# Shifted attention scores on masks preset by ScalarE and VectorE, in fixed pairs of PSUM banks

## The chip, the cores and the metric

The kernel runs on one core of a Trainium2 chip. The metric is the device time of one execution in microseconds. The median of three runs of the kernel before is 666.25 us (665.54 to 667.37).

## The reference

One block of a transformer with adaptive layer norms, on x of 4 batch rows x 512 tokens x 256 features, all in float32:

- `mod = silu(c) @ wmod` gives six vectors per batch row: two shifts, two scales, two gates.
- `h = layernorm(x) * (1 + ca) + sa`, then an attention block on h: rmsnorm, a projection to q, k and v with 32 heads of 8 features, rotary embedding of q and k, scores `q k^T / sqrt(8)`. A score is masked where the key is later than the query or lies in another of the four blocks of 128 tokens; then softmax, `@ v`, the output projection, and a gated MLP of width 512 with its own rmsnorm. `x += ga * result`.
- `h = layernorm(x) * (1 + cb) + sb`, then a gated feed-forward of width 704 with low-rank experts: a softmax router over 8 experts picks two of rank 16, and the result is `x += gb * (...)`.

For this change only the attention scores matter. Since the mask cuts the sequence into four blocks of 128 tokens, each of 32 heads in each of four blocks is a causal 128 x 128 softmax.

## The kernel before

A program written out engine by engine: each engine has its own instruction stream in source order, and semaphores (`Signal`) join them. The four batch rows are processed one after another, with the preparation of the next row woven into the current one.

**Attention units.** A row has `UNITS` = 8 units: two halves of the heads (16 heads) times four blocks of 128 tokens. A unit handles 16 heads as four groups of four heads, two groups at a time: `n = 2u + a` with a in 0, 1 counts the parts. For each part TensorE computes the scores twice.

- `scores_for_max` (L1546): two mask matmuls (`masked`, L1531: identity x mask in bf16, 512 columns, `start=True`) and two score matmuls of K = 32 in different row tiles, from rounded q and k, into one pair of PSUM banks. VectorE (`unit_max`, L1135) reduces 1024 columns to 8 negated maxima. When both parts are done, TensorE transposes the maxima (`max_transposed`, L1564, four 128-column transpositions) and ScalarE copies them as additional rows into the stacked queries (`max_to_rows`, L773). These scores run `AHEAD` = 2 units ahead.
- `shifted_scores` (L1579): with the maxima in the contraction (K = 100), again two mask matmuls and two score matmuls of 512 columns into a pair of banks. ScalarE takes the exponential of 1024 columns into `prob[a]` (L807; in units 6 and 7 the first part in two halves, L802 and L804).
- `contexts` (L1598): 16 matmuls of 128 columns in column tiles of width 32 per part (the trace counts 64 per unit and not 32, since each float32 matmul is issued twice) accumulate values and denominators in bank 6. VectorE's `normalise` (L1151) takes a reciprocal and a product.
- GpSimd spreads queries, keys and values for units to come (`spread_queries`, L570).

**Slots.** Three pairs of banks serve as slots (`slot`, L360): slot 0 is banks 2 and 3, slot 1 banks 4 and 5, slot 2 banks 0 and 1. The list `fills` (L349 to L357) has every use of a slot in TensorE's order: maximum scores `s1`, transposition `t`, shifted scores `s2`. Before, they rotate through the three slots. `fill` (L1522) makes TensorE wait until the earlier use of the same slot was read: `max_done` (VectorE) for s1, `max_rows` (ScalarE) for t, `exp_done` (ScalarE) for s2.

**TensorE's order in a unit.** Shifted scores of part 0, maximum scores (two units ahead) of part 0, the same two for part 1, contexts of part 0, contexts of part 1, transposition of the maxima. After that: in unit 2 the mean of the next row (L1437), in unit 4 its mean of squares, in unit 5 the spreading of its 1/std (not in the last row).

**The other queues in a unit.** ScalarE: two exponentials; in unit 0 a copy of h; `max_to_rows`; in row 0 further casts in units 0 and 1 (`high_parts`, `chunk_high`); in units 3 and 6 the squares of the next row (`front_squares`, L706), which wait for VectorE's centring. VectorE: two reductions; in row 0, unit 2, `chunk_low`; in unit 3 `centre` (L1042), in unit 6 `front_scale`; then `normalise`.

Of the kernel before, what the change touches and what calls it, by code (L numbers as in the profile page):

```python
# [32 lines left out]
P = 128  # L33
# [69 lines left out]
CHUNK_WIDTHS += [SPLIT_COLS - sum(CHUNK_WIDTHS) - 2 * S, 2 * S]  # L103
CHUNKS = [(sum(CHUNK_WIDTHS[:c]), width) for c, width in enumerate(CHUNK_WIDTHS)]
LATE_CHUNK = 4
FIRST_CONST = CONST["ident"][0]


# [53 lines left out]
def adaln_kernel(nc, x, smalls, wmod, wsplit, wplain, consts, masks, out):  # L162
    with ExitStack() as ctx:
# [167 lines left out]
        lora_hi = signal("lora_hi", 4)  # L331
        powers_set = signal("powers_set", 1)
        exp_half = signal("exp_half", 2)
        lora_lo = signal("lora_lo", 4)
        gu_ready = signal("gu_ready", FT * VARIANTS)
        ff_silu = signal("ff_silu", FT * VARIANTS)
# [14 lines left out]
        for u in range(UNITS):  # L351
            for a in range(2):
                fills += [("s2", 2 * u + a)] + ([("s1", 2 * (u + AHEAD) + a)] if u + AHEAD < UNITS else [])
            if u + AHEAD < UNITS:
                fills += [("t", u + AHEAD)]
        for n, what in enumerate(fills[6:]):
            slot_of[what] = (n + 2) % 3  # L357
        freed_by = {"s1": max_done, "t": max_rows, "s2": exp_done}

        def slot(fill):  # L360
# [307 lines left out]
        def _(act):  # L668
# [104 lines left out]
            def max_to_rows(row, u, ahead):  # L773
# [4 lines left out]
                nc.scalar.copy(q_st[MROW:KS, half * GQ:(half + 1) * GQ, blk * P:(blk + 1) * P], src)\  # L778
                    .then_inc(max_rows.sem, 1)

            def tails_stacked():

                act.wait_ge(chunk_hi[5].sem, 1)
                act.wait_ge(chunk_lo[5].sem, 1)
                for name, width in (("wd", D), ("ad", E * R)):
                    at = KEPT[name] + (FT - 1) * width
                    nc.scalar.copy(w_lo[TAIL:P, at:at + width], w_hi[0:TAIL, at:at + width].bitcast(F32))\
                        .then_inc(tail_stacked.sem, 1)

            def row_steps(row, last):  # L790

                for u in range(UNITS):
                    for a in range(2):
                        n = 2 * u + a
                        act.wait_ge(s2_ready.sem, s2_ready.count(row, n + 1))
                        if n >= 2:

                            act.wait_ge(pv_done.sem, pv_done.count(row, n - 1))
                        scores = slot(("s2", n)).rearrange("p a s -> p (a s)")
                        if u + AHEAD >= UNITS and a == 0:  # L800

                            nc.scalar.activation(prob[a][:, 0:S], scores[:, 0:S], ACT.Exp, scale=SCALE)\  # L802
                                .then_inc(exp_half.sem, 1)
                            nc.scalar.activation(prob[a][:, S:2 * S], scores[:, S:2 * S], ACT.Exp, scale=SCALE)\  # L804
                                .then_inc(exp_done.sem, 1)
                        else:
                            nc.scalar.activation(prob[a], scores, ACT.Exp, scale=SCALE).then_inc(exp_done.sem, 1)  # L807
                        if row == n == 0:
                            max_to_rows(0, 1, 0)
                    if u == 0:  # L810

                        act.wait_ge(out_ready.sem, out_ready.count(row, 0))
                        act.wait_ge(front.shifted.sem, front.shifted.count(row, 1))
                        nc.scalar.copy(h[:], h_next[:]).then_inc(h_moved.sem, 1)
                    if u + AHEAD < UNITS:
                        max_to_rows(row, u + AHEAD, 0)
                    if row == 0:

                        if u == 0:
                            act.wait_ge(rope_hi.sem, 4)  # L820
                            high_parts(3)
                            high_parts(2)
                        elif u == 1:
                            chunk_high(LATE_CHUNK)
                        elif u == 4:
                            tails_stacked()
                    if not last and u in (3, 6):
                        front_squares(row, 0 if u == 3 else 1, 1)
# [145 lines left out]
        def _(dve):  # L974
# [172 lines left out]
            def row_steps(row, is_last):  # L1147
# [19 lines left out]
                for u in range(UNITS):  # L1167
                    if not is_last and u == 5:
                        variance(0, row)
                    if u + AHEAD < UNITS:  # L1170
                        unit_max(row, u + AHEAD, 0)
                    if row == 0 and u == 2:
                        chunk_low(LATE_CHUNK)
                    if not is_last:
# [241 lines left out]
        def _(pe):  # L1416
# [160 lines left out]
            def row_steps(row, is_last):  # L1577

                def shifted_scores(n):  # L1579
                    u, a = n // 2, n % 2  # L1580
                    blk, half = u % BLOCKS, u // BLOCKS
                    if a == 0:
# [3 lines left out]
                            half_stacked(pe, row, half, 0)  # L1586
                        if u == BLOCKS:
                            pe.wait_ge(ones_back.sem, 16)
                    to = fill(row, "s2", n, 0)
                    for g in range(2):  # L1590
                        masked(to[:, g, :], 2)
                    for g in range(2):
                        gq = 2 * a + g
                        last = nc.tensor.matmul(to[:, g, :], k_st[0:KS, half * GQ + gq, blk * P:(blk + 1) * P],  # L1594
                                                q_ex[u % 2][0:KS, gq], start=False, stop=True)
                    last.then_inc(s2_ready.sem, 1)

                def contexts(n):  # L1598
# [29 lines left out]
                    shifted_scores(0)  # L1628
                max_transposed(row, 1, 0)
                for u in range(UNITS):  # L1630
                    for a in range(2):
                        if row or u or a:
                            shifted_scores(2 * u + a)
                        if u + AHEAD < UNITS:
                            scores_for_max(row, 2 * (u + AHEAD) + a, 0)
                    for a in range(2):
                        contexts(2 * u + a)
                    if u + AHEAD < UNITS:
                        max_transposed(row, u + AHEAD, 0)
                    if not is_last:  # L1640

# [384 lines left out]
```

## Time and profile before

| | |
|---|---|
| median of 3 runs | 666.25 us (665.54 to 667.37) |
| the profiled execution | 665.03 us, of which the span is 663.2 us |
| TensorE's mean granted clock | 0.978 of full speed |
| TensorE | 619.9 us busy, 93% of the span, 5816 matmuls |
| TensorE's weight loads | 424.9 us, beside its matmuls |
| VectorE | 404.6 us, 61%, 623 instructions |
| ScalarE | 315.7 us, 48%, 478 instructions |
| GpSimd | 185.2 us, 28%, 264 instructions |
| mask matmuls (L1532) | 256, 77.9 us busy |

Times are microseconds unless marked ns. A matmul's duration in the trace holds the latency of the array, and matmuls overlap: what one costs is the distance from its start to the next one's start. In the view in order of time, a row gives the start, the time until the group's end, the engine and the line; in brackets is the idle time of the engine before it and what ended it. "PE" is the matmul and "PEld" the load of its weights.

### The profile page before, as it was taken

Reading aid. Unit: us, or ns where it says so; the run is one execution under the profiler, and the core shown is the slowest. Engines: PE = TensorE matmul, PEld = TensorE weight load, DVE = VectorE, ACT = ScalarE, POOL = GpSimd, SP = SyncE. Lnnn points to the kernel's source line nnn. Section 1 sums busy time; section 2 is a strip of 40 time slices with the busy share of each in tenths; the row PEclk is TensorE's granted clock in tenths of the full one; section 3 lists DMA queues with packets and bytes.
Section 4 is the critical chain, followed back from the end, with each engine's and each line's share of the span. In section 5 each row is a group of like instructions: output and inputs, shape, how many; then the busy total and the mean of one; then the engine's idle time right before and its main releaser. Section 6 shows DMA issues by size and latency. Waiting matters only on the chain.

```text
span 663.2 us, 13983 instructions
## 1 busy us (share of the span) xinstructions
PE 619.9 (93%) x5816; PEld 424.9 (64%) x5816; DVE 404.6 (61%) x623; ACT 315.7 (48%) x478; POOL 185.2 (28%) x264
## 2 busy tenths in 40 slices
PE   5689999999999999999999999999999999869996
PEld 3545667567864667667884657766785566637783
DVE  2786744687467563668557555468647664447554
ACT  3736464356444356257443445437534444417442
POOL 1156640024016561034005662023102763000000
PEclk8599999999999999999999999999999999989999
DMA  8744000034022000025012100004202100000000
GB/s 327 239 111 119 30 3 1 1 83 109 1 60 99 2 2 3 0 48 144 1 27 70 64 3 2 1 14 123 57 0 64 65 2 3 1 1 0 1 1 32
DMA packets 16456, 31.77 MB, mean 48 GB/s; under 512 B 5060, under 2 KB 5828, under 8 KB 16260
## 3 DMA queue, kind: packets, MB, share of 16 engines
q1 hardware_dynamic: 14856, 27.98, 14.5%
q0 software_dynamic: 1152, 2.36, 1.4%
q8 instruction: 46, 0.75, 0.5%
q10 hardware_dynamic: 384, 0.52, 0.3%
q14 instruction: 18, 0.15, 0.1%
HBM read 12.99 MB, written 2.10 MB: 23 GB/s over the span
## 4 chain that ended last, share of the span: by engine, by line
PE 72%; DVE 14%; ACT 9%; issue 4%; DMA 1%; DVEq 0%; SPq 0%; ACTq 0%
PE bank L1622 8%; PE bank L1532 7%; PE bank L1424 5%; PE bank L1428 5%; PE bank L1425 5%; PE bank L1710 4%; PE bank L1560 3%; PE bank L1594 3%; PE bank L1805 3%; PE bank L1807 3%; PE bank L1568 3%; PE bank L1806 3%; PE bank L1831 2%; PE bank L1828 2%; PE bank L1464 2%
## 5 line engine op out<-in xcount | busy, mean ns | idle before, releaser
L1143 DVE TENSOR_REDUCE neg_max<-bank 128x8 f32<-128x1024 f32 x64 | 77.7, 1223 | 46.5 <-PE bank L1560 46.3
L584 POOL TENSOR_SCALAR arena_r<-q_st,const 100x512 fp32r<-100x512 f32 x128 | 87.7, 702 | 47.5 <-ACT q_st L778 47.1
L1332 DVE TENSOR_TENSOR arena<-arena,bank 128x512 f32<-128x512 f32 (+1 forms) x72 | 49.6, 688 | 71.7 <-ACT arena L870 69.9
L1424 PE MATMUL bank<-n_hi,w_lo 128*128 128x512 f32 x184 | 79.8, 434 | 3.3 <-ACT n_hi L733 1.7
L870 ACT ACTIVATE arena<-bank 128x512 f32<-128x512 f32 (+1 forms) x72 | 43.0, 598 | 82.0 <-PE bank L1807 47.0
L1532 PE MATMUL bank<-mask 128*128 128x512 bf16 x256 | 77.9, 386 | 3.6 <-ACT n_hi L683 2.2
L1428 PE MATMUL bank<-n_lo,w_hi 128*128 128x512 f32 x184 | 74.4, 404 | 0.2
L1425 PE MATMUL bank<-n_hi,w_hi 128*128 128x512 f32 x184 | 74.1, 403 | 0.0
L807 ACT ACTIVATE tile_f<-bank 128x1024 f32<-128x1024 f32 x56 | 57.2, 1024 | 33.4 <-PE bank L1594 33.2
L565 POOL TENSOR_TENSOR k_wide<-n_lo,head_of 128x512 fp32r<-128x512 f32 x30 | 32.6, 1089 | 103.9 <-DMA n_lo<-k_st 103.9
L539 POOL TENSOR_TENSOR tile_f<-tile_f,const 128x512 f32<-128x512 f32 x16 | 22.3, 1394 | 121.5 <-ACT tile_f L719 121.5
L1622 PE MATMUL bank<-tile_f,v_ex 128*32 128x128 f32 x1024 | 52.5, 276 | 1.5 <-ACT tile_f L807 1.5
L1317 DVE TENSOR_TENSOR arena_r<-arena,arena_r 128x512 fp32r<-128x512 f32 (+1 forms) x72 | 51.3, 715 | 3.8 <-ACT arena_r L885 2.9
L1161 DVE RECIPROCAL arena<-bank 128x128 f32<-128x128 f32 x32 | 30.6, 957 | 37.2 <-PE bank L1622 37.2
L1594 PE MATMUL bank<-arena_r,k_st 100*128 100x512 f32 x128 | 52.9, 494 | 0.0
L778 ACT CAST q_st<-bank 4x512 fp32r<-4x512 f32 x32 | 18.5, 578 | 71.7 <-PE bank L1568 71.7
L1622 PE MATMUL bank<-tile_f,ones_ex 128*32 128x128 f32 x1024 | 51.6, 273 | 0.0
L885 ACT CAST arena_r<-arena 128x512 fp32r<-128x512 f32 (+1 forms) x72 | 44.0, 613 | 10.6 <-DVE arena L1332 3.9
L1424 PEld LDWEIGHTS bank<-n_hi,w_lo 128*128 128x128 f32 x184 | 35.4, 192 | 15.6 <-ACT n_hi L739 4.2
L1428 PEld LDWEIGHTS bank<-n_lo,w_hi 128*128 128x128 f32 x184 | 35.4, 192 | 10.3 <-DVE n_lo L1072 1.8
L1425 PEld LDWEIGHTS bank<-n_hi,w_hi 128*128 128x128 f32 x184 | 35.6, 193 | 8.5 <-issue 1.7
L1805 PE MATMUL bank<-arena_r,w_lo 128*128 128x512 f32 (+1 forms) x96 | 38.5, 401 | 2.6 <-DVE arena_r L1309 2.1
(180 smaller groups left out, 1167.9 us busy)
## 6 DMA issues: line engine op xcount, KB each, us to landing
q_st<-arena_r SPq DMA_DIRECT2D x96, 64.0 KB, 2.0
k_st<-arena_r SPq DMA_DIRECT2D x52, 64.0 KB, 2.0
k_st<-arena_r POOLq DMA_DIRECT2D x36, 64.0 KB, 2.4
h_next<-in_x SPq DMA_DIRECT2D x4, 512.0 KB, 3.6
tile_f<-in_x SPq DMA_DIRECT2D x4, 512.0 KB, 4.4
out<-arena SPq DMA_DIRECT2D x4, 512.0 KB, 2.8
n_lo<-k_st SPq DMA_DIRECT2D x24, 64.0 KB, 2.0
n_hi<-q_st SPq DMA_DIRECT2D x24, 64.0 KB, 2.0
```

The costliest lines, as they stand in the source:

```text
L584: last = nc.gpsimd.tensor_scalar(q_ex[u % 2][0:KS, :, hh, :], src, con("head")[0:KS, hh:hh + 1], 1.0, ALU.mult, ALU.mult)
L807: nc.scalar.activation(prob[a], scores, ACT.Exp, scale=SCALE).then_inc(exp_done.sem, 1)
L1143: nc.vector.tensor_reduce(neg_max[:, 2 * a:2 * a + 2, MROW:KS], slot(("s1", n)).rearrange("p a (h s) -> p a h s", s=P), AX_X, ALU.max, neg ...
L1317: nc.vector.tensor_tensor(to, pair_tmp[j % 2][0:width], ff_hl[j % 4][0][0:width].bitcast(F32), ALU.subtract)\
L1332: nc.vector.tensor_tensor(pair_tmp[n % 2][0:width], silu_out[n % 2][0:width], up, ALU.mult)\
L1424: nc.tensor.matmul(to, wl[:, at], n_hi[:, kt, :], start=kt == 0, stop=False)
L1425: nc.tensor.matmul(to, wh[:, at], n_hi[:, kt, :], start=False, stop=False)
L1428: last = nc.tensor.matmul(to, wh[:, at], n_lo[:, kt, :], start=False, stop=kt == KT - 1)
L1532: nc.tensor.matmul(to, mask[:, 0, :], mask[:, which:which + 1, :].broadcast_to([P, GH, P]), start=True, stop=False)
L1594: last = nc.tensor.matmul(to[:, g, :], k_st[0:KS, half * GQ + gq, blk * P:(blk + 1) * P], q_ex[u % 2][0:KS, gq], start=False, stop=True)
L1622: last = nc.tensor.matmul(tile, weights, prob[a][:, at:at + P], start=a == j == kind == 0, stop=a == j == 1, skip_group_check=True)
L1805: nc.tensor.matmul(to, wl[:, cols], ah, start=False, stop=False, skip_group_check=True)
```

## The change

- In units 1 to 6 (`PRESET`) `shifted_scores` issues no mask matmuls. The mask is written to the pair of banks beforehand: for part 0 by ScalarE (`preset`, after the two exponentials of the unit before), for part 1 by VectorE (a `tensor_copy` after `unit_max` and ahead of the rest of the unit's work). Each writes 1024 float32 columns from a bf16 mask that is broadcast, and waits for the exponential that reads the pair last. TensorE waits for `mask_set[a]`, and its score matmuls then accumulate on what stands there. Units 0 and 7 keep the mask matmuls.
- Slots: shifted scores of part 0 always use slot 2 (banks 0 and 1), those of part 1 slot 1 (banks 4 and 5). All maximum scores and transpositions from unit 0 on use slot 0 (banks 2 and 3).
- TensorE's order in a unit: shifted scores 0, maximum scores 0, shifted scores 1, contexts 0, maximum scores 1, contexts 1, transposition.

```diff
--- before.py
+++ after.py
@@ -103,6 +103,7 @@
 CHUNK_WIDTHS += [SPLIT_COLS - sum(CHUNK_WIDTHS) - 2 * S, 2 * S]
 CHUNKS = [(sum(CHUNK_WIDTHS[:c]), width) for c, width in enumerate(CHUNK_WIDTHS)]
 LATE_CHUNK = 4
+PRESET = range(1, UNITS - 1)
 FIRST_CONST = CONST["ident"][0]
 
 
@@ -331,6 +332,7 @@
         lora_hi = signal("lora_hi", 4)
         powers_set = signal("powers_set", 1)
         exp_half = signal("exp_half", 2)
+        mask_set = [signal(f"mask_set{a}", len(PRESET)) for a in range(2)]
         lora_lo = signal("lora_lo", 4)
         gu_ready = signal("gu_ready", FT * VARIANTS)
         ff_silu = signal("ff_silu", FT * VARIANTS)
@@ -353,8 +355,8 @@
                 fills += [("s2", 2 * u + a)] + ([("s1", 2 * (u + AHEAD) + a)] if u + AHEAD < UNITS else [])
             if u + AHEAD < UNITS:
                 fills += [("t", u + AHEAD)]
-        for n, what in enumerate(fills[6:]):
-            slot_of[what] = (n + 2) % 3
+        for kind, n in fills[6:]:
+            slot_of[kind, n] = 2 - n % 2 if kind == "s2" else 0
         freed_by = {"s1": max_done, "t": max_rows, "s2": exp_done}
 
         def slot(fill):
@@ -778,6 +780,12 @@
                 nc.scalar.copy(q_st[MROW:KS, half * GQ:(half + 1) * GQ, blk * P:(blk + 1) * P], src)\
                     .then_inc(max_rows.sem, 1)
 
+            def preset(row, n):
+
+                act.wait_ge(exp_done.sem, exp_done.count(row, n - 1))
+                to = slot(("s2", n)).rearrange("p g (h s) -> p (g h) s", s=P)
+                nc.scalar.copy(to, mask[:, 2:3, :].broadcast_to([P, 2 * GH, P])).then_inc(mask_set[0].sem, 1)
+
             def tails_stacked():
 
                 act.wait_ge(chunk_hi[5].sem, 1)
@@ -807,6 +815,8 @@
                             nc.scalar.activation(prob[a], scores, ACT.Exp, scale=SCALE).then_inc(exp_done.sem, 1)
                         if row == n == 0:
                             max_to_rows(0, 1, 0)
+                    if u + 1 in PRESET:
+                        preset(row, 2 * (u + 1))
                     if u == 0:
 
                         act.wait_ge(out_ready.sem, out_ready.count(row, 0))
@@ -1169,6 +1179,11 @@
                         variance(0, row)
                     if u + AHEAD < UNITS:
                         unit_max(row, u + AHEAD, 0)
+                    if u + 1 in PRESET:
+
+                        dve.wait_ge(exp_done.sem, exp_done.count(row, 2 * u + 2))
+                        nc.vector.tensor_copy(slot(("s2", 2 * u + 3)).rearrange("p g (h s) -> p (g h) s", s=P),
+                                              mask[:, 2:3, :].broadcast_to([P, 2 * GH, P])).then_inc(mask_set[1].sem, 1)
                     if row == 0 and u == 2:
                         chunk_low(LATE_CHUNK)
                     if not is_last:
@@ -1586,13 +1601,19 @@
                             half_stacked(pe, row, half, 0)
                         if u == BLOCKS:
                             pe.wait_ge(ones_back.sem, 16)
-                    to = fill(row, "s2", n, 0)
-                    for g in range(2):
-                        masked(to[:, g, :], 2)
+                    if u in PRESET:
+
+                        pe.wait_ge(mask_set[a].sem, mask_set[a].count(row, u - PRESET[0] + 1))
+                        to = slot(("s2", n))
+                    else:
+                        to = fill(row, "s2", n, 0)
+                        for g in range(2):
+                            masked(to[:, g, :], 2)
                     for g in range(2):
                         gq = 2 * a + g
                         last = nc.tensor.matmul(to[:, g, :], k_st[0:KS, half * GQ + gq, blk * P:(blk + 1) * P],
-                                                q_ex[u % 2][0:KS, gq], start=False, stop=True)
+                                                q_ex[u % 2][0:KS, gq], start=False, stop=True,
+                                                skip_group_check=u in PRESET)
                     last.then_inc(s2_ready.sem, 1)
 
                 def contexts(n):
@@ -1628,14 +1649,17 @@
                     shifted_scores(0)
                 max_transposed(row, 1, 0)
                 for u in range(UNITS):
-                    for a in range(2):
-                        if row or u or a:
-                            shifted_scores(2 * u + a)
-                        if u + AHEAD < UNITS:
-                            scores_for_max(row, 2 * (u + AHEAD) + a, 0)
-                    for a in range(2):
-                        contexts(2 * u + a)
-                    if u + AHEAD < UNITS:
+                    further = u + AHEAD < UNITS
+                    if row or u:
+                        shifted_scores(2 * u)
+                    if further:
+                        scores_for_max(row, 2 * (u + AHEAD), 0)
+                    shifted_scores(2 * u + 1)
+                    contexts(2 * u)
+                    if further:
+                        scores_for_max(row, 2 * (u + AHEAD) + 1, 0)
+                    contexts(2 * u + 1)
+                    if further:
                         max_transposed(row, u + AHEAD, 0)
                     if not is_last:
```

## Rows read from the trace of the kernel before

**Rows 1.** The busy shares of the page: busy us (share of the span) xinstructions of each engine.

```profile
PE 619.9 (93%) x5816; PEld 424.9 (64%) x5816; DVE 404.6 (61%) x623; ACT 315.7 (48%) x478; POOL 185.2 (28%) x264
```

**Rows 2.** Stretches of row 1, then row 0: length, busy us of each engine, PEclk, DMA.

```profile
205.51:211.57 6.06, 6.06 (x85) 3.69 (x84) 3.86 (x4) 3.56 (x4) 4.90 (x7) 1.00 0.23 89
211.57:217.69 6.12, 6.12 (x88) 3.74 (x84) 3.70 (x4) 2.62 (x3) 4.09 (x6) 1.00 0.53 174
223.81:231.64 7.83, 7.83 (x92) 4.42 (x89) 4.24 (x6) 2.62 (x3) 4.09 (x6) 1.00 0.01 2
231.64:238.03 6.39, 6.27 (x89) 3.74 (x85) 4.26 (x6) 3.75 (x5) 4.09 (x6) 1.00 0.01 3
238.03:244.89 6.86, 6.86 (x152) 4.29 (x148) 3.79 (x5) 2.62 (x3) 4.11 (x6) 1.00 0.01 2
244.89:250.43 5.54, 5.38 (x88) 3.97 (x85) 2.66 (x4) 3.64 (x6) 3.09 (x5) 1.00 0.00 0
55.54:61.92 6.38, 6.28 (x88) 3.73 (x85) 3.70 (x4) 3.76 (x5) 4.38 (x7) 1.00 0.39 91
61.92:68.90 6.98, 6.27 (x88) 3.73 (x85) 4.25 (x5) 4.26 (x4) 4.10 (x6) 1.00 0.62 177
```

**Rows 3.** One unit of row 1 in order: start us, us, engine line op.

```profile
217.69 0.64 PE L1568 MATMUL bank<-const,neg_max 128*100 128x128 f32 x4
...
218.37 0.58 ACT L778 CAST q_st<-bank 4x512 fp32r<-4x512 f32 x1 [2.32 <-PE bank L1568]
...
219.08 0.61 PE L1532 MATMUL bank<-mask 128*128 128x512 bf16 x2
...
220.05 0.60 PE L1532 MATMUL bank<-mask 128*128 128x512 bf16 x2
...
220.96 0.61 PE L1532 MATMUL bank<-mask 128*128 128x512 bf16 x2
...
221.92 0.43 PE L1622 MATMUL bank<-tile_f,v_ex 128*32 128x128 f32 x8
...
222.04 1.23 DVE L1143 TENSOR_REDUCE neg_max<-bank 128x8 f32<-128x1024 f32 x1 [0.59 <-PE bank L1560]
...
223.81 0.64 PE L1568 MATMUL bank<-const,neg_max 128*100 128x128 f32 x4
```

**Rows 4.** Order of time: a transposition that waited, and a matmul behind narrow ones.

```profile
203.06 2.35 DVE L1143 TENSOR_REDUCE neg_max<-bank 128x8 f32<-128x1024 f32 x2
...
205.51 0.60 PE L1568 MATMUL bank<-const,neg_max 128*100 128x128 f32 x4
...
206.15 0.58 ACT L778 CAST q_st<-bank 4x512 fp32r<-4x512 f32 x1 [3.60 <-PE bank L1568]
...
259.27 0.50 PE L1673 MATMUL bank<-n_hi,w_lo 128*128 128x512 f32 x1 [0.20 <-ACT n_hi L833]
...
259.84 0.39 PE L1673 MATMUL bank<-n_hi,w_lo 128*128 128x512 f32 x1
```

**Rows 5.** Order of time: centring, squares, exponential; contexts that waited.

```profile
231.01 1.27 DVE L1046 TENSOR_TENSOR h_next<-h_next,bank 128x512 f32<-128x512 f32 x2
...
232.92 1.15 ACT L689 ACTIVATE arena<-h_next 128x512 f32<-128x512 f32 x2
...
234.10 1.02 ACT L807 ACTIVATE tile_f<-bank 128x1024 f32<-128x1024 f32 x1
...
249.42 0.43 PE L1622 MATMUL bank<-tile_f,v_ex 128*32 128x128 f32 x8 [0.16 <-ACT tile_f L807]
```

**Rows 6.** Groups by line and form: a copy and two splits of weights, busy and mean ns.

```profile
L1286 DVE COPY arena<-pick 128x512 f32<-128x512 f32 x8 | 3.0, 420 | 0.0
...
L1029 DVE TENSOR_TENSOR w_lo<-arena,w_hi 128x1856 fp32r<-128x1856 f32 x1 | 2.1, 2082 | 0.0
...
L678 ACT CAST w_hi<-arena 128x1856 fp32r<-128x1856 f32 x1 | 1.7, 1741 | 0.0
```

**Rows 7.** The stretch before the clock fell in row 0, columns as in rows 2.

```profile
43.70:47.10 3.40, 1.28 (x6) 0.43 (x6) 1.29 (x3) 2.23 (x4) 2.61 (x4) 1.00 0.37 87
```

## The prediction

> **What bounds the kernel now.** I read first the busy shares: TensorE 93% of the span, every other engine 61% or less [rows 1]. Then I cut row 1 of the batch into its attention units; unit u here runs from the transposition that precedes it to the next one [rows 2]. In units 0, 1, 3 and 5 the PE column equals the length of the window; only unit 4 (0.12 us) and unit 6 (0.16 us) leave it idle, while VectorE works 3.7 us and ScalarE 2.6 us of 6.12. So TensorE's own work sets a unit, and an instruction taken off it is worth its time as long as no result that it waits for comes too late. Then I read a unit in order of time [rows 3]: shifted scores with their masks take 0.91 (220.05 to 220.96), maximum scores 0.97 (219.08 to 220.05), both halves' contexts 1.89 (221.92 to 223.81), four transpositions 0.48. The wait that is nearest to being late is the maximum: the second reduction starts at 222.04, ends at 223.27, and the transposition that needs it comes at 223.81.
>
> **What goes.** Six units x two halves x two masks x four rows are 96 of the 256 mask matmuls. A pass of 512 columns is 0.91/4 = 0.23 us, so 0.45 per half and 0.91 per unit; all of it, 96 x 0.23 = 21.8 us, would come off if nothing else bound.
>
> **What comes in its place.** Every maximum score and every transposition now uses one pair of banks (slot 0), where three pairs rotated. So three waits that had a unit's slack lie in one chain: the first maximum scores wait for ScalarE's copy of the last transposition, the second ones for the first reduction, the transposition for the second. I add up that chain from one transposition to the next.
> - Transposition to copy: 0.64 (205.51 to 206.15) and 0.58; with a wake-up of 0.05 (a reduction ends at 205.41, TensorE loads at 205.46) TensorE starts the first maximum scores at 1.27. It has then worked 0.44 + 0.48 (transposition, first shifted scores without masks), so it stands idle for 0.35 [rows 3, 4].
> - First maximum scores 0.97, to 2.24.
> - Second shifted scores, now in front of the contexts: two passes, 0.47, and 0.11 because no mask hides their weight load behind narrow tiles (the first 512-column matmul after narrow ones takes 0.50, the later ones 0.39 [rows 4]). 0.58, to 2.82. Bounds: 0.47 if the load is hidden, 0.66 if all 0.19 shows.
> - Contexts of the first half by themselves: 1.01 (249.42 to 250.43, the window's end) [rows 2, 5], since entering and leaving narrow tiles is paid for each half; 0.94 is the lower bound. To 3.83. The first reduction is done at 2.24 + 0.17 + 1.22 + 0.05 = 3.68, just in time.
> - Second maximum scores 0.97, to 4.80.
> - Then 0.11 to the reduction (221.92 to 222.04), 1.23 for it, 0.10 to the transposition (205.41 to 205.51): 1.43. The second contexts cover 1.01 of it. The next transposition stands at 6.23.
>
> Against 6.12 now a unit is 0.11 **longer** although 0.91 of masks is gone: 0.24 goes to exposed loads and the split contexts, 0.77 to the two new waits (0.35 and 0.42).
>
> **The presets.** ScalarE: 1024 columns, at the 1.02 of its exponential [rows 5]. It follows the second exponential (2.82 + 0.20 + 1.02 = 4.04) and ends at 5.06, before the next shifted scores at 6.67; at double the price it would still be hidden. Behind it in ScalarE's queue is only the copy for the next transposition, at 6.87. VectorE: no copy into PSUM is in the trace. Above stands the reduction of 1024 elements, 1.23, or 1.14 in a row since two overlap by 0.1 [rows 4]; below, twice the 512-element copy of 0.42 [rows 6], 0.76 in a row. I take 1.14, as the row that touches the same memory. The Trainium skill ("VectorE: DVE Perf Modes", section "Why PSUM operands drop a tier") says that fp32 with an operand in PSUM runs at one element a cycle; that sides with the upper value, and no row here shows such a copy. In a plain unit VectorE has 3.70 + 1.14 = 4.84 of 6.23, but the preset stands ahead of the normalisation and of what is put before that: the reduction ends at -0.10, preset to 1.04, normalisation (3.70 less two reductions, 1.25) to 2.29, ahead of the contexts at 2.82 and of the next reduction at 2.41. Hidden there, with 0.1 to spare.
>
> **Units that differ (rows 1 and 2 of the batch).**
> - Unit 0 keeps its masks: the first maximum scores start at 0.44 + 0.91 = 1.35, the second shifted scores are 0.91: 6.23 + 0.08 + 0.33 = 6.64 against 6.06: +0.57.
> - Units 1, 2: +0.11 each.
> - Unit 3: the mean matmuls (1.72) hide ScalarE's copy. The maximum scores start at 0.48 + 1.72 + 0.48 = 2.67, which gives 6.23 + 1.40 = 7.63 against 7.83: -0.20.
> - Unit 4 is the expensive one. Centring of the next row (1.27) is queued on VectorE behind the new preset, ScalarE's squares (1.15) wait for it, and the exponential is queued behind the squares [rows 5]. Now centring ends at 232.28, 0.64 after the transposition. After: -0.10 + 1.14 + 1.27 = 2.31; squares to 3.51, exponential to 4.56, contexts at 4.61 instead of 2.82. 6.23 + 1.79 = 8.02 against 6.39: +1.63 (+1.25 with the cheap preset).
> - Unit 5: squares' mean and shifted scores bring the maximum scores to 1.80: 6.76 against 6.86: -0.11.
> - Unit 6 has no maximum scores; its end hangs on three exponentials after the first shifted scores, which come 0.43 earlier without masks: 5.11 against 5.54: -0.43.
> - Unit 7 keeps its masks: 0.
>
> Sum +1.68 per row, twice: +3.36. The last row has no next row to prepare: 0.57 + 5 x 0.11 - 0.36 = +0.76 (unit 6 there gains 0.36 and not 0.43, since the copy for the last transposition holds ScalarE until 1.22). Row 0 has further ScalarE casts (3.76 - 2.62 = 1.14 in unit 1, 1.74 in unit 2) ahead of the first exponential and now in the chain: 1.22 + 1.14 + 1.05 + 0.05 = 3.46 and 4.04 instead of 2.82 give 6.88 and 7.45 against 6.38 and 6.98, +0.50 and +0.47; VectorE's split of 2.08 in unit 3 adds about 0.40 [rows 2, 6]. Row 0: 0.57 + 0.50 + 0.47 + 0.20 + 1.63 - 0.11 - 0.43 = +2.83.
>
> Together 3.36 + 0.76 + 2.83 = **+7.0 us**. The profiled execution took 665.03 (its span 663.20, 1.8 around it), so 672.0; it lies 1.2 below the median of 666.25, so I predict a median of **673.2**.
>
> **Range of this case.** Twenty units hang on the chain. Load hidden (-0.11) and contexts at 0.94 (-0.07): -3.6; cheap preset three times 0.38: -1.1; so 668.5. Load fully exposed (+0.08), copy 0.68 instead of 0.64 (as at 218.37), reduction 0.17 after its scores instead of 0.11: +3.6: 677.
>
> **Rivals.**
> - *The single pair doesn't bind and TensorE's order does.* Then a unit is its work: 0.44 + 0.48 + 0.97 + 0.58 + 1.01 + 0.97 + 1.01 = 5.46, -0.66 in units 1 to 5, unit 6 -0.43: some -3.8 per row, 651. For it: in the trace of before nothing waits for these results within a plain unit. Against: 1.43 from scores to transposition stands against 1.01 of cover, and 1.27 for the copy against 0.92, all measured. It decides as soon as a unit falls under about 5.9. 0.11.
> - *Unit 4's side chain isn't lengthened* (a cheap preset, or centring early): 3 x 1.63 goes, 668.3, on the border of no change. 0.10.
> - *The clock falls.* In unit 4 TensorE would stand for 1.8 us on end. The one time in row 0 that the clock went to half, TensorE had been busy 1.28 of 3.40 us [rows 7]; unit 4 would have some 5.5 of 8.0. A stretch of 3.4 us at 1.2 GHz costs up to 1.7 in each of three rows: 678. 0.09. The Trainium skill ("TensorE: Matmul & The Clock Gate", section "A second HAM failure mode: psum-queue depth-cycling") warns that short frequent idling between groups of matmuls makes the clock swing; by it every plain unit is in danger. The waits here of 0.35 and 0.42 are of that kind; no run shows them yet.
> - The forecast: 0.70.
>
> What a measurement of this kernel tells from no change is about 0.3%, 664.3 to 668.3. Faster 0.11 (the first rival); same 0.09 (most of the second); slower 0.80. The range 667 to 677.5 leaves out the first rival and the far end of the third.
>
> **What will show it.** Idle time of TensorE before its first maximum-score mask, ended by ScalarE's copy, about 0.35 a unit; before the transposition, ended by VectorE's reduction, about 0.42. Plain units of 6.2; unit 4 at 8.0 with the contexts waiting for an exponential that starts behind the squares; unit 6 at 5.1. VectorE's preset 1.2, ScalarE's 1.0. It is wrong if plain units come out under 6.0, or if the presets cost much more or less than these rows.

## The result

| | before | changed |
|---|---|---|
| median | 666.81 us (4 runs) | 676.52 us (4 runs) |
| ratio | | 1.0153, 95% interval 1.0123 to 1.0183 |
| span of the profiled execution | 663.2 us | 673.9 us |

Slower by 1.5%; the forecast was 1.0%. The spans differ by 10.7 us. The busy shares after, against [rows 1]: TensorE does 8.4 us less and stands idle 19 us more.

```profile
PE 611.5 (91%) x5720; PEld 412.7 (61%) x5720; DVE 428.5 (64%) x647; ACT 337.7 (50%) x502; POOL 185.9 (28%) x264
```

The windows that answer to [rows 2] in the same order (length, busy us of PE, PEld, DVE, ACT, POOL, clock, DMA share and rate): units 0, 1, 3, 4, 5 and 6 of row 1, then units 1 and 2 of row 0. The reader is to compare the length with PE's busy time, its first number: they were equal in most units of before, and are 0.7 apart in unit 1 now (6.45 and 5.76), and 2.2 in unit 4.

```profile
208.52:215.28 6.76, 6.36 (x86) 3.66 (x85) 4.00 (x5) 4.51 (x5) 5.21 (x8) 1.00 0.20 80
215.28:221.73 6.45, 5.76 (x80) 3.21 (x81) 4.73 (x6) 3.54 (x4) 4.04 (x7) 1.00 0.49 163
228.18:235.91 7.73, 7.33 (x85) 3.96 (x85) 4.73 (x6) 3.54 (x4) 4.11 (x7) 1.00 0.01 2
235.91:243.91 8.00, 5.81 (x80) 3.23 (x81) 5.83 (x8) 4.59 (x6) 4.10 (x7) 1.00 0.00 0
243.91:250.77 6.86, 6.45 (x145) 3.85 (x145) 4.81 (x7) 3.55 (x4) 4.12 (x7) 1.00 0.01 4
250.77:255.85 5.08, 4.53 (x80) 3.55 (x81) 3.44 (x5) 3.64 (x6) 2.81 (x5) 1.00 0.01 3
56.17:63.22 7.05, 5.82 (x80) 3.24 (x81) 4.73 (x6) 4.57 (x6) 4.04 (x7) 1.00 0.43 92
63.22:70.87 7.65, 5.81 (x80) 3.24 (x81) 4.73 (x6) 5.18 (x5) 4.17 (x7) 1.00 0.39 138
```

| unit | before | predicted | after | row 0 before | predicted | after |
|---|---|---|---|---|---|---|
| 0 | 6.06 | 6.64 | 6.76 | 5.69 | 6.26 | 6.55 |
| 1 | 6.12 | 6.23 | 6.45 | 6.38 | 6.88 | 7.05 |
| 2 | 6.12 | 6.23 | 6.45 | 6.98 | 7.45 | 7.65 |
| 3 | 7.83 | 7.63 | 7.73 | 7.83 | 8.03 | 7.80 |
| 4 | 6.39 | 8.02 | 8.00 | 6.39 | 8.02 | 8.01 |
| 5 | 6.86 | 6.76 | 6.86 | 6.86 | 6.75 | 6.84 |
| 6 | 5.54 | 5.11 | 5.09 | | | |

The units 0 to 5 of all rows are 11.9 us longer together, unit 6 is 0.45 shorter in three rows and 0.33 in the last: 10.2 of the 10.7 us are in the attention units. The rest lies elsewhere: row 2 loses 0.8 behind its attention units, ahead of the matmuls of L1439, for a reason that was not followed up; the start of row 0 gains 1.2 up to its first transposition and loses 1.0 again up to the second, and the clock was at half for 6.8 us there against 20.5 before. Unit 0 of row 0 ran its first 1.4 us at half clock, against 0.7 before.

A plain unit in order of time, which answers to [rows 3]: the transposition, ScalarE's copy, the first mask, the second shifted scores, the reductions, VectorE's preset, the next transposition's weight load.

```profile
221.73 0.61 PE L1583 MATMUL bank<-const,neg_max 128*100 128x128 f32 x4 [0.40 <-DVE neg_max L1153]
...
222.38 0.58 ACT L780 CAST q_st<-bank 4x512 fp32r<-4x512 f32 x1 [2.07 <-PE bank L1583]
...
223.11 0.59 PE L1547 MATMUL bank<-mask 128*128 128x512 bf16 x2 [0.29 <-ACT q_st L780]
...
224.06 0.73 PE L1614 MATMUL bank<-arena_r,k_st 100*128 100x512 f32 x2
224.24 1.23 DVE L1153 TENSOR_REDUCE neg_max<-bank 128x8 f32<-128x1024 f32 x1 [0.34 <-PE bank L1575]
...
225.73 0.61 PE L1547 MATMUL bank<-mask 128*128 128x512 bf16 x2
...
226.81 1.23 DVE L1153 TENSOR_REDUCE neg_max<-bank 128x8 f32<-128x1024 f32 x1 [1.34 <-PE bank L1575]
...
227.95 1.22 DVE L1185 CAST bank<-mask 128x1024 f32<-128x1024 bf16 x1
228.15 0.39 PEld L1583 LDWEIGHTS bank<-const,neg_max 128*100 128x100 f32 x4 [0.64 <-DVE neg_max L1153]
```

Two brackets name the two waits: TensorE stands 0.29 until ScalarE's copy (L780) has ended, and before the transposition 0.40 (its load 0.64) until the reduction (L1153) has. Together they are the 0.69 that TensorE is idle in the unit. In [rows 3] neither row had a bracket of that kind. The third wait that was forecast, of the second maximum scores for the first reduction, stays hidden: that reduction ends at 225.47, and the contexts keep TensorE until the mask at 225.73.

Unit 4, against [rows 5]: VectorE's preset (L1185), centring (L1056), ScalarE's squares (L691), exponentials (L815), contexts.

```profile
235.68 1.22 DVE L1185 CAST bank<-mask 128x1024 f32<-128x1024 bf16 x1
...
236.81 1.27 DVE L1056 TENSOR_TENSOR h_next<-h_next,bank 128x512 f32<-128x512 f32 x2
...
238.11 1.15 ACT L691 ACTIVATE arena<-h_next 128x512 f32<-128x512 f32 x2 [0.98 <-DVE h_next L1056]
...
239.29 1.94 ACT L815 ACTIVATE tile_f<-bank 128x1024 f32<-128x1024 f32 x2
...
240.46 0.43 PE L1643 MATMUL bank<-tile_f,v_ex 128*32 128x128 f32 x8 [1.50 <-ACT tile_f L815]
```

Each begins where the one above it ends (236.90, 238.08, 239.26; the contexts follow the first of the two exponentials), and the contexts find TensorE idle for 1.50.

### The profile page after: what moved, and what is told of

Its sections match the earlier page's. It is cut to its first block, busy times and chain, and to the rows that moved or that the text cites. A ratio compares the mean times of both kernels' runs of the same rounds, so it can differ in the third digit from the quotient of the medians.

```text
span 673.9 us, 13839 instructions
## 1 busy us (share of the span) xinstructions
PE 611.5 (91%) x5720; PEld 412.7 (61%) x5720; DVE 428.5 (64%) x647; ACT 337.7 (50%) x502; POOL 185.9 (28%) x264
## 4 chain that ended last, share of the span: by engine, by line
PE 63%; DVE 19%; ACT 9%; issue 5%; SPq 3%; DMA 1%; POOL 0%; DVEq 0%; ACTq 0%; POOLq 0%
PE bank L1547 5%; DVE neg_max L1153 5%; PE bank L1439 5%; PE bank L1443 5%; PE bank L1440 4%; PE bank L1643 4%; PE bank L1734 4%; PE bank L1575 3%; PE bank L1614 3%; PE bank L1829 3%; SPq L416 3%; PE bank L1831 2%; PE bank L1830 2%; PE bank L1583 2%; PE bank L1479 2%
## 5 line engine op out<-in xcount | busy, mean ns | idle before, releaser
L1153 DVE TENSOR_REDUCE neg_max<-bank 128x8 f32<-128x1024 f32 x64 | 77.6, 1222 | 51.7 <-PE bank L1575 51.6
L586 POOL TENSOR_SCALAR arena_r<-q_st,const 100x512 fp32r<-100x512 f32 x128 | 89.4, 718 | 58.8 <-ACT q_st L780 58.5
L1439 PE MATMUL bank<-n_hi,w_lo 128*128 128x512 f32 x184 | 79.4, 431 | 3.5 <-ACT n_hi L735 1.7
L815 ACT ACTIVATE tile_f<-bank 128x1024 f32<-128x1024 f32 x56 | 56.9, 1025 | 27.0 <-PE bank L1614 26.6
L1547 PE MATMUL bank<-mask 128*128 128x512 bf16 x160 | 49.7, 393 | 6.4 <-ACT q_st L780 4.0
L780 ACT CAST q_st<-bank 4x512 fp32r<-4x512 f32 x32 | 18.5, 579 | 66.2 <-PE bank L1583 66.1
L1614 PE MATMUL bank<-arena_r,k_st 100*128 100x512 f32 x128 | 48.4, 464 | 0.0
L1439 PEld LDWEIGHTS bank<-n_hi,w_lo 128*128 128x128 f32 x184 | 35.2, 191 | 15.9 <-ACT n_hi L741 4.2
L1643 PEld LDWEIGHTS bank<-tile_f,v_ex 128*32 128x32 f32 x1024 | 25.6, 109 | 29.3 <-issue 25.5
```

The source lines that it names most:

```text
L586: last = nc.gpsimd.tensor_scalar(q_ex[u % 2][0:KS, :, hh, :], src, con("head")[0:KS, hh:hh + 1], 1.0, ALU.mult, ALU.mult)
L1153: nc.vector.tensor_reduce(neg_max[:, 2 * a:2 * a + 2, MROW:KS], slot(("s1", n)).rearrange("p a (h s) -> p a h s", s=P), AX_X, ALU.max, neg ...
L1439: nc.tensor.matmul(to, wl[:, at], n_hi[:, kt, :], start=kt == 0, stop=False)
L1547: nc.tensor.matmul(to, mask[:, 0, :], mask[:, which:which + 1, :].broadcast_to([P, GH, P]), start=True, stop=False)
L1643: last = nc.tensor.matmul(tile, weights, prob[a][:, at:at + P], start=a == j == kind == 0, stop=a == j == 1, skip_group_check=True)
```

## The experiments

All are timed beside the kernel before on the same chip. "Changed" is the changed kernel; a plain unit is one that has nothing but attention in it (units 1 and 2, in the last row 1 to 5), and takes 6.45 there. The first four undo parts of the change.

**e1: slots and order without presets.**

```diff
-PRESET = range(1, UNITS - 1)
+PRESET = range(0)
```

> New slots and new order of TensorE, but no presets: the mask matmuls are back in all eight units. My theory (a unit is the chain copy, maximum scores, reduction, maximum scores, reduction, transposition): the masks of the first shifted scores lie in the wait for ScalarE's copy and cost nothing, those of the second add 0.25 to a plain unit (6.45 to 6.70), unit 4 gets shorter since VectorE's preset no longer stands ahead of the centring (8.0 to 6.9); in all about 681. Rival, the presets themselves cost the time (writes that delay others): below the changed kernel, near 670.

Measured 682.44, ratio 1.0243 (1.0228 to 1.0257). Plain units 6.79, unit 4 7.06. The two parts of the change other than the presets make the kernel slower by 2.4%; the presets give a third of it back.

**e2: TensorE's order alone.** As e1, and the slots rotate again:

```diff
-        for kind, n in fills[6:]:
-            slot_of[kind, n] = 2 - n % 2 if kind == "s2" else 0
+        for n, what in enumerate(fills[6:]):
+            slot_of[what] = (n + 2) % 3
```

> Only TensorE's new order: masks by matmul everywhere and the three pairs of banks rotating as before. My theory in its measured terms: the transposition follows the second maximum scores by 1.49 with only the second contexts (1.01) between, so a plain unit is 0.44 + 0.91 + 0.95 + 0.91 + 1.01 + 0.97 + 1.49 = 6.68, the same as with the single pair: about 681. Rival, the single pair of banks is what costs and the order is harmless: near the kernel before, 667 to 669.

Measured 679.56, ratio 1.0204 (1.0186 to 1.0222), plain units 6.72. The order by itself costs 13 us, with banks as they were. So a version that splits the contexts loses its cover for the second reduction whatever the banks are: TensorE stands 0.32 before the transposition here too. The single pair adds only 0.07 a unit as long as the masks are there to fill the wait for the copy. The prediction had put both waits down to the single pair; the one before the transposition belongs to the order.

**e3: neither masks nor presets in units 1 to 6.** The presets of ScalarE and VectorE and their waits are taken out, and the first score matmul starts the bank:

```diff
-q_ex[u % 2][0:KS, gq], start=False, stop=True,
+q_ex[u % 2][0:KS, gq], start=u in PRESET, stop=True,
```

> The changed kernel with neither presets nor masks in units 1 to 6 (those scores stay unmasked, and the exponential's scale is 0.05 of what it was so that it stays finite). My theory: plain units stay at 6.45, since no preset is on the chain; only unit 4 falls from 8.0 to 6.9, as the centring is no longer queued behind the preset: 3 x 1.1 less, about 673. Rival, the presets collide or hold up their engines in every unit: plain units under 6.1 and less than 665.

Measured 673.70, ratio 1.0104 (1.0088 to 1.0120). Plain units 6.44, unit 4 7.05. (Row 0's unit 2 took 9.21 in this trace, with the clock at half for 3.4 us of it, and 7.65 in the changed kernel.) Even when the masks cost nothing on any engine the kernel isn't faster than before. In plain units the presets are free; in unit 4 they cost 0.95.

**e4: TensorE's order of before, with presets and the single pair.**

```diff
-                    contexts(2 * u)
                     if further:
                         scores_for_max(row, 2 * (u + AHEAD) + 1, 0)
+                    contexts(2 * u)
                     contexts(2 * u + 1)
```

> The changed kernel with TensorE's order of before (both maximum scores ahead of the contexts). My theory: the second maximum scores wait for the first reduction with only the second shifted scores between, and both contexts follow: 1.37 + 0.95 + 1.52 + 0.97 + 1.89 = 6.70 in a plain unit, 0.25 more than now, about 680. Rival, the new order is what costs: faster than the changed kernel, about 668.

Measured 678.30, ratio 1.0182 (1.0144 to 1.0221, runs from 673.4 to 682.9). Plain units 6.66. Given the single pair, the new order is the better one by 0.2 in a plain unit: the contexts between the two maximum scores hide the first reduction, for which TensorE stands 1.09 here. It isn't better everywhere. Unit 4 is 7.00 here and 8.00 in the changed kernel, and row 0's units 1 and 2 are 6.67 each against 7.05 and 7.65; the two profiled executions are equally long (673.8 and 673.9), and the intervals of the two ratios overlap. As a whole these runs don't tell which order is better. Order and single pair each lengthen a plain unit: the order without the pair in e2, the pair with the old order here, though with the presets in place; no run has the pair and the old order with masks by matmul.

This trace also shows the clock fall in the middle of plain units. In unit 2 of the last row, TensorE's busy time (first number after the length) in one stretch and the granted clock (the third number from the end) in the next:

```profile
533.94:537.35 3.41, 2.11 (x8) 0.72 (x8) 1.77 (x3) 2.58 (x4) 3.17 (x5) 1.00 0.01 2
537.35:540.76 3.41, 3.41 (x51) 2.65 (x54) 2.36 (x2) 0.46 (x1) 0.52 (x1) 0.50 0.02 5
```

The first stretch holds the two stops of every plain unit of this kernel, 0.29 for the copy and 1.09 for the reduction; the unit took 8.57 and not 6.66. The other plain units, with the same stops, kept the full clock. Whether more such falls make the runs differ by 9.5 us isn't known, since one execution of them was profiled.

The next ones go the other way, each on top of the one before it.

**e5: centring early.** `centre` is called ahead of `unit_max` in unit 3.

```diff
+                    if not is_last and u == 3:
+                        centre(front, row, 1, h_next, h_next)
                     if u + AHEAD < UNITS:
                         unit_max(row, u + AHEAD, 0)
```

> The changed kernel with one move on VectorE: in unit 3 the centring of the next row comes before the two reductions instead of after them and the preset. My theory: it runs in VectorE's idle time behind the mean, the squares start right behind ScalarE's copy, and unit 4 falls from 8.0 to about 6.5; three rows, 4.6 less than the changed kernel, about 672. Rival, unit 4 is long for another reason (the reduction held up by the normalisation): it stays above 7.3 and the time above 674.

Measured 673.51, ratio 1.0123 (1.0106 to 1.0141), 0.003 less than the changed kernel's, with intervals that overlap; the gain is seen in the unit. Unit 4 is 7.06 and not 6.5; in row 0 unit 3 grew to 9.01, since there the centring stands behind the split of weights and now holds up the reductions. The rows of unit 4 in row 1: the squares still stand ahead of the first exponential, which begins 2.43 after the transposition (at 236.42) and frees the contexts at 3.59, where a plain unit of the changed kernel has them at 2.99.

```profile
237.67 1.15 ACT L691 ACTIVATE arena<-h_next 128x512 f32<-128x512 f32 x2
...
238.85 1.94 ACT L815 ACTIVATE tile_f<-bank 128x1024 f32<-128x1024 f32 x2
```

That is what I had left out: of the 1.55 that unit 4 is longer than a plain unit in the changed kernel, the preset ahead of the centring was 0.95 (8.00 against 7.05 in e3), the squares ahead of the exponential 0.6.

**e6: transpositions in bank 7.** Units 0, 1 and 3 (in the last row all) transpose into bank 7, which the next row's norm uses only in between, so slot 0 is free as soon as the reduction is done.

```diff
+        def apart(row, u):
+            return u in ((2, 3, 5) if row < B - 1 else range(2, UNITS))
...
+                if apart(row + ahead, u):
+                    pe.wait_ge(max_rows.sem, max_rows.count(row, u, ahead))
+                    if u == 5 and row < B - 1:
+                        pe.wait_ge(front.centred.sem, front.centred.count(row, 1, 1))
+                    to = t_bank(row + ahead, u)
```

> As the early centring, and the transpositions of units 0, 1 and 3 (in the last row all six) go to bank 7, so that the maximum scores no longer wait for ScalarE's copy. My theory: in these units the wait of 0.45 before the maximum scores goes, a plain unit takes 0.92 + 0.95 + 0.66 + 1.01 + 0.97 + 1.49 = 6.0; about 14 such units, 6 less than the early centring alone, about 666. Rival, the chain through the reductions takes up what is freed: 671 or more.

Measured 670.43, ratio 1.0066 (1.0050 to 1.0082). Plain units 5.95 (6.05 where the transposition at the end still uses slot 0), as worked out (6.0): the wait for the copy is gone, and 0.3 before the transposition is left. The sum of 14 such units was too hopeful: nine got shorter. Units 0, 3, 4 and 5 stay within 0.1 of what they were, and so do row 0's units 1 and 2.

**e7: those transpositions after the next unit's first shifted scores.**

```diff
                     if row or u:
                         shifted_scores(2 * u)
+                    if u and apart(row, u + 1):
+                        max_transposed(row, u + 1, 0)
```

> As before with bank 7, and these transpositions are issued after the next unit's first shifted scores, which cover the reduction's end. My theory: TensorE's own work would give 5.6, but VectorE (reduction, preset, normalisation, 3.7 after the last maximum scores) holds the next contexts and reduction by some 0.4: a plain unit is about 5.9 to 6.0 and the time 663 to 666. Rival, VectorE has room enough: 5.6 and about 660.

Measured 672.87, ratio 1.0096 (1.0072 to 1.0121): no gain. Plain units 5.97, as expected; whether for the reason given, e8 tells. The time was not as expected (663 to 666). In the trace units 0 and 3 are 0.2 longer than in e6, and in row 0 the clock went to half twice in the attention units (at 68.8 and 85.9, for 3.4 us each), which e6's did not.

**e8: both presets on ScalarE.**

```diff
-.then_inc(mask_set[0].sem, 1)
+.then_inc(mask_set[n % 2].sem, 1)
...
                         preset(row, 2 * (u + 1))
+                        preset(row, 2 * (u + 1) + 1)
```

> As the later transposition, and ScalarE writes both presets. My theory: ScalarE has 4.7 of work in a unit, none of it late, VectorE is back at 3.7, and a plain unit is TensorE's own 5.6: about 659, faster than the kernel before by 1%. Rival, ScalarE becomes the bound since the exponentials queue behind two presets and the copy: 6.0 or more and no gain over the version with one preset on each.

Measured 672.15, ratio 1.0094 (1.0075 to 1.0114). Plain units 5.97 again, where 5.6 and 659 were expected: VectorE was not what held e7 up, and that theory falls. The rival (6.0, no gain, the exponentials queue on ScalarE) has the number; the queue, though, is behind the copy alone. The trace shows what did: transposition, ScalarE's copy (L788), exponentials (L823).

```profile
542.52 0.60 PE L1594 MATMUL bank<-const,neg_max 128*100 128x128 f32 x4
...
543.16 0.58 ACT L788 CAST q_st<-bank 4x512 fp32r<-4x512 f32 x1 [1.56 <-PE bank L1594]
...
543.76 1.95 ACT L823 ACTIVATE tile_f<-bank 128x1024 f32<-128x1024 f32 x2
```

The first exponential starts 1.24 after the transposition, though its scores were done before the transposition. ScalarE's queue is in order, the copy stands ahead of the exponential, and the copy now waits for a transposition that was moved behind those scores. It is the same kind of wait as the squares in unit 4.

The same trace shows the clock. In unit 4 of row 1, columns as in e4's:

```profile
237.80:241.20 3.40, 1.94 (x22) 0.95 (x24) 1.52 (x2) 3.33 (x5) 2.64 (x4) 1.00 0.00 0
241.20:244.60 3.40, 3.40 (x40) 1.71 (x36) 0.50 (x1) 2.19 (x3) 1.06 (x2) 0.50 0.00 0
```

It was busy 1.94 of 3.40 us, and the next stretch ran at half clock, 1.2 GHz; unit 4 took 8.29, and 7.04 in e7, where the clock held. Row 0 shows it twice and row 2 once. The profiled execution of the changed kernel kept the full clock in every attention unit after row 0's start, also in its unit 4, although it was busy there for 1.68 of the 3.41 us from 237.05 to 240.46, less than here.

**e9: the copy after the first exponential.** And the squares behind unit 4's exponentials.

```diff
+                        if a == 0 and u and apart(row, u + 1):
+                            max_to_rows(row, u + 1, 0)
+                    if not last and u == 4:
+                        front_squares(row, 0, 1)
...
-                    if u + AHEAD < UNITS:
+                    if u + AHEAD < UNITS and not apart(row, u + AHEAD):
                         max_to_rows(row, u + AHEAD, 0)
```

> As both presets on ScalarE, and ScalarE copies a transposition in bank 7 after the next unit's first exponential instead of before it; the squares of the next row move behind unit 4's exponentials. What the trace of the version before it shows: with the copy in front, the exponential starts 1.24 after the transposition and the contexts wait for it, 5.97 a unit with 5.6 of TensorE's work. My theory: the wait goes, plain units take 5.6 and unit 4 under 7: 14 x 0.35 + 3 x 1.4 less, 661 to 663, faster than the kernel before by 0.5%. Rival, the next wait behind it (GpSimd's queries, 4.1 after the copy) takes its place: 5.9 and about 668.

Measured 660.52, ratio 0.9930 (0.9913 to 0.9947): faster than both kernels. Plain units 5.61, unit 4 5.51. Not all of the 11.6 us against e8 is the queue: e8's trace has four falls of the clock in the attention units and this one has none. In unit 4 of row 1, 1.25 of the 2.78 that it got shorter is the clock, by e7. In its rows the exponential starts 0.20 after the transposition and the copy follows it; the last row is the next transposition, 5.60 on. TensorE is busy for all of the 5.60.

```profile
529.31 0.60 PE L1598 MATMUL bank<-const,neg_max 128*100 128x128 f32 x4
...
529.51 1.02 ACT L823 ACTIVATE tile_f<-bank 128x1024 f32<-128x1024 f32 x1 [0.77 <-PE bank L1629]
...
530.55 0.58 ACT L788 CAST q_st<-bank 4x512 fp32r<-4x512 f32 x1
...
534.91 0.60 PE L1598 MATMUL bank<-const,neg_max 128*100 128x128 f32 x4
```

**e10: the same with the second preset on VectorE.**

> The same with the second preset on VectorE as in the change. My theory: VectorE's reduction, preset and normalisation end 3.7 after the last maximum scores where the next contexts come at 3.5, so plain units take 5.8 to 5.9, about 665; VectorE is the worse place for the second preset once the chain is shorter. Rival, VectorE has room: the same as with both on ScalarE.

Measured 661.99, ratio 0.9953 (0.9935 to 0.9971). Plain units 5.80: now VectorE's queue does bind, by 0.2, as was said too early of e7. The time is 3 less than expected; against e9 it is 1.5 more, with intervals that just overlap.

**e11: the same without presets**, all masks by matmul.

> The same arrangement of banks, order and queues with no presets: all masks by matmul. It prices the presets where the chain no longer binds. My theory: TensorE's work is then the unit, 5.6 less 0.2 of exposed loads plus 0.91 of masks, 6.3: slower than both the version with presets (by about 10 in all) and the kernel before, some 671. Rival, masks are hidden in waits here too: within 2 of the version with presets.

Measured 673.76, ratio 1.0127 (1.0109 to 1.0146). Plain units 6.29 (6.3 expected), and units 0 and 3 are 0.3 and 1.1 longer than in e9. Against e9 the presets are worth 2.0%, 13 us. That is the saving that the change aimed at, though not the 21.8 us of all its masks: it is there once no wait of the single pair lies on the path of a plain unit.

## Why the prediction was right, point by point

- **Direction: right. Mechanism: right in what decides the unit, with one part put down to the wrong cause.** Two waits decide it, for the copy (e6 takes it away) and for the second reduction (e4, e9); the third stayed hidden, as worked out. The 0.91 of masks is lost in them and in the contexts' split (e3). But only the first comes of the single pair. The second comes of TensorE's new order: e2 has it with the three pairs rotating, 0.32 of 0.40.
- **The size of a plain unit: short by 0.22** (6.23 predicted, 6.45 measured, in some twenty units). By its terms, from the rows of the plain unit above: transposition to first mask 1.38 against 1.27 (223.11 - 221.73), of which 0.12 is between the copy's end at 222.96 and the load of the mask at 223.08, where 0.05 was taken, and 0.03 from that load to its matmul, which the prediction left out here; first maximum scores 0.95 against 0.97; second shifted scores with the way into the contexts 0.66 against 0.58; contexts 1.01 as taken; second maximum scores 0.97; to the transposition 1.48 against 1.43, where the load comes 0.11 after the reduction's end (228.15 against 228.04) and the model row showed 0.05 (205.46 against 205.41) [rows 4]. So three terms were too small: the way from the copy to the mask by 0.11, the exposed load by 0.08, the way from the scores to the transposition by 0.05. The load came out at its upper bound, 0.66. The first and the third are mostly the wake-up after a wait, for which 0.05 was taken; no bound was given for it, and the 6.45 lies above the 6.41 that the upper bounds allow for a unit. For the third the last section shows what makes it longer; for the first no run does.
- **Unit 4: right**, 8.02 against 8.00, and by the chain described: the contexts come 4.55 after the transposition (4.61 predicted). The terms that were too small lie beside that chain, so it escaped them. e3 prices the preset in it at 0.95, e5 the squares at 0.6.
- **Units 0, 3, 5, 6.** In rows 1 and 2, units 0 and 3 have the sign right and are 0.1 longer than worked out; unit 6 is as said. Unit 5 was to get 0.1 shorter and didn't (6.86 before and after). In row 0, unit 3 was to get 0.20 longer and didn't (7.80 against 7.83): the 0.40 for VectorE's split isn't there. Unit 0 there is 0.29 longer than predicted, with 0.7 us more of it at half clock. The 4.04 for row 0's unit 2 is 4.06 by its own terms, and nothing hangs on it.
- **Presets.** VectorE's copy takes 1.22, the upper bound I had taken, and ScalarE's 1.02:

```profile
L1185 DVE CAST bank<-mask 128x1024 f32<-128x1024 bf16 x24 | 29.2, 1217 | 0.0
```

```profile
L787 ACT CAST bank<-mask 128x1024 f32<-128x1024 bf16 x24 | 24.5, 1021 | 0.0
```

  The rule of the Trainium skill ("VectorE: DVE Perf Modes", section "Why PSUM operands drop a tier"), one float32 element a cycle with an operand in PSUM, agrees with 1217 ns for 1024 columns, where twice the 512-column copy of 420 ns would have been 840: the cheap preset was no case.
- **Rival 1 (the pair doesn't bind, a unit is TensorE's own work)** would have needed a unit below 5.9. It fails in the changed kernel, and e9 shows what it asks for: 5.61, near its 5.46.
- **Rival 2 (unit 4's side chain isn't lengthened)** didn't come. Its price was too high: with the presets gone (e3) or the centring early (e5) unit 4 is 7.05 and 7.06, so 0.95 goes and not 1.63, as the squares stay ahead of the exponential.
- **Rival 3 (the clock)** did not come in the profiled execution of the changed kernel, but did in e3, e4, e7 and e8. It cost 1.25 in e8's unit 4 and 1.91 in e4's plain unit (8.57 against 6.66), where up to 1.7 was taken; that its chance of 0.09 was too low is my reading. The Trainium skill ("TensorE: Matmul & The Clock Gate", section "A second HAM failure mode: psum-queue depth-cycling") would have had the short waits of every plain unit swing the clock. The changed kernel's trace doesn't show that, the stops of 0.29 and 0.40 left it at full speed; e4's trace shows it once, over stops of 0.29 and 1.09.
- **The sum**: 7.0 predicted in the attention units, 10.2 there in the trace. It is 3.2 short, almost all of one sign: the same short terms went into nearly every unit. The median rose by 9.7. It lies in the range although plain units came out above their upper bound, because unit 4 took no part in that and row 0's unit 3 had been overstated; this much of the hit is luck.

## What to carry to other kernels

Taking work off the busiest engine pays only if the buffers that are rearranged for it do not tie what used to run a unit apart: write the chain down from one occurrence of the shared buffer to the next, and compare it with the engine's own work, before and after. Give a buffer with a short life (here a transposition) its own place, and in every in-order queue put the instruction whose input comes last behind those whose inputs are there. Together with the centring moved early and the transposition moved behind the next scores, these turned 1.5% slower into 0.5% faster with the same presets (e10), and into 0.7% faster with both presets on ScalarE (e9).

## What the runs showed that was not expected

- From the second reduction's end to the load that follows were 0.11 to 0.12 in the changed kernel and 0.05 in the rows of before. The transposition waits for two things, its own reduction and the last read of its slot. In the changed kernel the slot was last read by that same reduction, so both conditions come true together; before, the slot's had come true earlier. e1 and e2 differ in nothing but the slots and show it, e1 first:

```profile
544.69 1.22 DVE L1153 TENSOR_REDUCE neg_max<-bank 128x8 f32<-128x1024 f32 x1 [1.69 <-PE bank L1575]
...
546.03 0.39 PEld L1583 LDWEIGHTS bank<-const,neg_max 128*100 128x100 f32 x4 [0.64 <-DVE neg_max L1153]
```

```profile
542.81 1.22 DVE L1153 TENSOR_REDUCE neg_max<-bank 128x8 f32<-128x1024 f32 x1 [1.69 <-PE bank L1575]
...
544.09 0.39 PEld L1583 LDWEIGHTS bank<-const,neg_max 128*100 128x100 f32 x4 [0.58 <-DVE neg_max L1153]
```

  From end to load it is 0.12 in e1 and 0.06 in e2 by these rows, and so in all 24 transpositions of units 2 to 7 of both traces (0.116 to 0.117 and 0.053 to 0.054 unrounded). That is 0.06 of the 0.07 a unit that the single pair costs in e1 over e2. In e6, transpositions into bank 7 show 0.05 and those into slot 0 in the same trace 0.12.
- In e9 a float32 score pair without masks costs 0.57 in front of a transposition and 0.65 in front of narrow tiles: the difference is read as a weight load that the masks used to cover, which no run measures by itself.
- The clock went to half after 1.46 us without work in 3.40 in e8, and after 1.30 in 3.41 in e4, and stayed full in the changed kernel over a single stop of 1.50.
